# First key weights loaded in two halves over both queues, and the last store split over two queues

## The chip, the cores and the metric

The kernel runs on one core of one Trainium2 chip. The metric is the device time of one execution in microseconds (us); lower is better. Each kernel was run several times and the median is what counts. Besides, one execution was recorded by the hardware profiler, and every row shown below comes from that one.

## The reference

Three residual blocks are applied to x, 256 rows of 512 values. The first is a cross attention over 4096 context rows, and only its beginning matters here:

```python
x = x + xattn(layernorm(x), ctx_2048, mask, Wq, bq, Wk, bk, Wv, bv, Wo, bo, gamma, beta, residual_scale)
x = x + latent_attention(layernorm(x), ...)       # 16 heads, causal
x = x + mixture_of_experts(layernorm(x), ...)     # 48 kept experts, top 8 per row

# in xattn, hs = layernorm(x), at = ctx_2048:
q = proj(hs, Wq, bq, S)
k = proj(at, Wk, bk, T)      # at @ Wk.T + bk
v = proj(at, Wv, bv, T)
```

The last block's result, added to x, is the output: 256 x 512 float32, stored as two tiles of 128 rows.

## The kernel before

Every engine has its own hand-written program, and semaphores order the work between them: `sp` (SyncE) issues most transfers, `act` (ScalarE) and `dve` (VectorE) convert and combine, `pool` (GpSimd) makes constants and does the power for the layernorm, `pe` (TensorE) multiplies. Products of float32 quality are made of three float16 products: each operand is split into a high and a low part (`wk16[:, 0]` and `wk16[:, 1]` for the key weights, `chi` and `clo` for the context), and PE adds high x high (k = 0), low x high (k = 1) and high x low (k = 2).

The start of the program, which most of the change touches, computes the keys of the first 512 context rows. The contraction over 512 channels is cut into four chunks c = 0 to 3 of 128. For each chunk SP loads the key weights `wk32[:, c]` (256 KB, line 301) and ACT's own queue loads the context `cbuf[:, 0, c]` (256 KB, line 451); both count on one semaphore, `first_in[c]`. SP's queue also carries x (512 KB, line 300, ahead of the fourth key weights), and behind them the query weights, the value weights and the next context block, 1 MB each. When `first_in[c]` is full:

- ACT makes the high part of the key weights (line 471, `wk_hi`) and, from c = 1, that of the context (line 448, `ctx_hi`). For c = 0 DVE makes the latter (line 794).
- DVE makes the low parts, that of the weights (line 790, `wk_lo`) and that of the context (line 780, `ctx_lo`), chunk by chunk for c = 0, 1, 2. Behind these it computes the layernorm statistics of x (lines 800 to 802), POOL takes the power (line 416), DVE makes the low parts of chunk 3 and then the normalised x (`xn`, line 807).
- PE first runs ten products of zeros (`zero16`) that nothing reads. Then for each chunk and each of k = 0, 1, 2 it runs four matmuls of 512 columns, one for each group n of 128 key channels, into four PSUM banks (pP, pD and the two of pO): 48 in all. Ahead of the last four, those of c = 3, k = 2, it transposes `xn` (line 1280). Then come the query projection, the values of the first block, and the attention loop.

At the end of the program the experts' sum lies in two PSUM banks. DVE copies the first to `work[:, 0]` and ACT the second to `work[:, 1]` (line 766); SP stores each with one transfer of 256 KB (lines 378 and 380) and waits for both. Matmuls go through the helper of line 1268, so most of PE's rows carry that line.

Of the kernel before, what the change touches and what calls it, by code (L numbers as in the profile page):

```python
# [13 lines left out]
TT, HC = T // 128, HID // 128  # L14
# [18 lines left out]
SA, SW, SH = 64.0, 256.0, 16.0  # L33
# [14 lines left out]
def build(nc, a, out):  # L48
    f32, f16, i32 = mybir.dt.float32, mybir.dt.float16, mybir.dt.int32
    ALU, ACT, AX = mybir.AluOpType, mybir.ActivationFunctionType, mybir.AxisListType  # L50

    ctx = ExitStack()
    with ctx:
        def sb(name, shape, dt=f32):
            return ctx.enter_context(nc.sbuf_tensor(name, shape, dt))

        def sem(name):
            return ctx.enter_context(nc.semaphore(name))
# [7 lines left out]
        def unit_bank(b, n):  # L66

            if isinstance(b, int) and b == 0:
                return (pP[:, :], pD[:, :], pO[:, 0, :], pO[:, 1, :])[n % 4]
            return pP[:, :]  # L70
# [10 lines left out]
        work = sb("work", [128, 2, HID])  # L81
# [38 lines left out]
        def take(n, dt=f32):  # L120
            words = n if dt == f32 else n // 2
            v = arena[:, at[0]:at[0] + words]
            at[0] += words
            assert at[0] <= ARENA
            return v if dt == f32 else v.bitcast(dt)


        cbuf = take(2 * HC * CB).rearrange("p (b c t) -> p b c t", b=2, c=HC)
# [3 lines left out]
        wk16 = take(2 * HC * HID, f16).rearrange("p (s c n) -> p s c n", s=2, c=HC)  # L132
# [15 lines left out]
        wk32, wv32 = (take(HC * HID).rearrange("p (c n) -> p c n", c=HC) for _ in range(2))  # L148
# [96 lines left out]
        wdram = nc.dram_tensor("w_scratch", [KEPT, T], f32, kind="Internal").ap()  # L245


        names = """x_in small_in row_in wq_in wv_in wo_in gate_in lat_in rope_in
            aux_in var_ready rstd_ready xn_ready tr_done xT_ready
            zero_ready const_ready zc_ready prep_ready wk_hi wk_lo wq_hi wq_lo xq_hi xq_lo q_mm q_f q_hi q_lo  # L250
            ctx_hi ctx_lo proj_done proj_evac k_lo
# [9 lines left out]
        s = {n: sem(n) for n in names}  # L261
        first_in = [sem(f"first_in{i}") for i in range(HC)]
# [11 lines left out]
        def _(sp):  # L274
# [23 lines left out]
            for c in range(HC):  # L298
                if c == HC - 1:
                    sp.dma_start(x_sb[:, :, :], a["x"]).then_inc(s["x_in"], 16)  # L300
                sp.dma_start(wk32[:, c], a["wkT"][:, c]).then_inc(first_in[c], 16)
            sp.dma_start(wqT, a["wqT"]).then_inc(s["wq_in"], 16)
            sp.dma_start(wv32, a["wvT"]).then_inc(s["wv_in"], 16)
            load_ctx(1, 1)
# [72 lines left out]
            sp.wait_ge(s["out0_ready"], 1)  # L377
            sp.dma_start(out[:, 0, :], work[:, 0, :]).then_inc(s["out_stored"], 16)
            sp.wait_ge(s["out1_ready"], 1)
            sp.dma_start(out[:, 1, :], work[:, 1, :]).then_inc(s["out_stored"], 16)  # L380
            sp.wait_ge(s["out_stored"], 32)


        @block.gpsimd
# [61 lines left out]
        def _(act):  # L446
            def split_ctx(p, c):
                act.activation(chi[:, p, c], cbuf[:, p, c], ACT.Copy, scale=SA).then_inc(s["ctx_hi"], 1)

            for c in range(HC):  # L450
                act.dma_start(cbuf[:, 0, c], a["ctxT"][0][:, c]).then_inc(first_in[c], 16)

            def evac(b, p, n):

# [12 lines left out]
                                   scale=1.0 / (SA * SW)).then_inc(s["proj_evac"], 1)  # L467

            for c in range(HC):
                act.wait_ge(first_in[c], 32)  # L470
                act.activation(wk16[:, 0, c], wk32[:, c], ACT.Copy, scale=SW).then_inc(s["wk_hi"], 1)  # L471
                if c == 1:
                    act.wait_ge(s["ctx_hi"], 1)
                if c:
                    split_ctx(0, c)
# [6 lines left out]
            for i in range(2):  # L482
                act.activation(xqh[:, 2 * i:2 * i + 2, :], pS[:, i, :].rearrange("p (c t) -> p c t", c=2), ACT.Copy,
                               scale=SA).then_inc(s["xq_hi"], 1)
# [116 lines left out]
            for t in range(TT):  # L601
                act.wait_ge(s["tr_done"], t + 2)
                act.activation(xh[:, :, 128 * t:128 * t + 128], pS[:, t, :].rearrange("p (c q) -> p c q", c=HC), ACT.Copy,
                               scale=SX).then_inc(s["xT_ready"], 1)
# [126 lines left out]
            for t in range(TT):  # L731
                cols = slice(128 * t, 128 * t + 128)
                rows = pS[:, 2 + t, :].rearrange("p (c q) -> p c q", c=HC)
# [30 lines left out]
            moe_units(UNITS // UNROLL - 1, last_turn=True)  # L764
            act.wait_ge(s["moe_done"], 2)
            act.activation(work[:, 1, :], pP[:, :], ACT.Copy, scale=1.0 / (SH * SW)).then_inc(s["out1_ready"], 1)


        @block.vector
        def _(dve):  # L770
# [15 lines left out]
                dve.tensor_tensor(kl[:, p, n], kf[:, n % 2], kh[:, p, n], ALU.subtract).then_inc(s["k_lo"], 1)  # L786

            def split_wk(n):
                dve.wait_ge(s["wk_hi"], n + 1)
                dve.scalar_tensor_tensor(wk16[:, 1, n], wk32[:, n], SW, wk16[:, 0, n], ALU.mult, ALU.subtract)\  # L790
                   .then_inc(s["wk_lo"], 1)

            dve.wait_ge(first_in[0], 32)
            dve.tensor_scalar(chi[:, 0, 0], cbuf[:, 0, 0], SA, None, ALU.mult).then_inc(s["ctx_hi"], 1)
            for n in range(HC - 1):
                split_wk(n)
# [24 lines left out]
                dve.scalar_tensor_tensor(xql[:, 2 * i:2 * i + 2, :], pS[:, i, :].rearrange("p (c t) -> p c t", c=2), SA,  # L821
                                         xqh[:, 2 * i:2 * i + 2, :], ALU.mult, ALU.subtract).then_inc(s["xq_lo"], 1)
            for c in range(HC):
                dve.wait_ge(s["wk_hi"], HC + c + 1)
                dve.scalar_tensor_tensor(wv16[:, 1, c], wv32[:, c], SW, wv16[:, 0, c], ALU.mult, ALU.subtract)\
                   .then_inc(s["wk_lo"], 1)
            for n in range(HC):
# [438 lines left out]
        def _(pe):  # L1266
            def mm(o, lhsT, rhs, start, stop, **kw):
                return pe.matmul(o, lhsT, rhs, start=start, stop=stop, **kw)  # L1268
# [7 lines left out]
            def transpose_rows(k):  # L1276
                pe.wait_ge(s["xn_ready"], k)
                for t in range(TT):
                    for c in range(HC):
                        last = pe.transpose(pS[:, c // 2, 256 * (c % 2) + 128 * t:256 * (c % 2) + 128 * t + 128],  # L1280
                                            xn[:, t, 128 * c:128 * c + 128], ident[:, :])
                last.then_inc(s["tr_done"], 1)

            def unit_part(bank, p, n, c, products=(0, 1, 2)):

                for k, (wi, ci) in enumerate(((0, chi), (1, chi), (0, clo))):
                    if k not in products:
                        continue
                    start, stop = c == 0 and k == 0, c == HC - 1 and k == 2
                    if n < HC:  # L1290
                        last = mm(bank, wk16[:, wi, c, 128 * n:128 * n + 128], ci[:, p, c, :], start, stop)
                    else:
                        r = n - HC
                        last = mm(bank, ci[:, p, c, 128 * r:128 * r + 128], wv16[:, wi, c, :], start, stop)
                if c == HC - 1 and 2 in products:
                    last.then_inc(s["proj_done"], 1)
# [24 lines left out]
                    tiled_part(p, n, c)  # L1321

            pe.wait_ge(s["zero_ready"], 1)
            for _ in range(10):
                mm(pS[:, 0, :], zero16[:, 0:128], zero16[:, :], True, True)
            for c in range(HC):
                for k in range(3):
                    if k == 0:
                        pe.wait_ge(s["wk_hi"], c + 1)
                        pe.wait_ge(s["ctx_hi"], c + 1)  # L1330
                    elif k == 1:
                        pe.wait_ge(s["wk_lo"], c + 1)
                    else:
                        pe.wait_ge(s["ctx_lo"], c + 1)
                    if c == HC - 1 and k == 2:
                        pe.wait_ge(s["const_ready"], 1)
                        transpose_rows(1)
                    for n in range(HC):
                        unit_part(unit_bank(0, n), 0, n, c, (k,))
            for k, (w, x) in enumerate(((wqh, xqh), (wql, xqh), (wqh, xql))):  # L1340
                for g in range(HC):
# [531 lines left out]
```

## Time and profile before

| | us |
|---|---|
| median of 3 runs | 715.83 |
| lowest and highest of them | 715.80, 716.37 |
| the profiled execution, its own time | 716.18 |
| its span, from the first to the last instruction | 714.3 |
| what lies around its span | 1.88 |

The profile is read from the page's busy shares first, then by the chain of waits and by the instructions in order of time in the first 25 us and the last 5 us, where the change is. Times in those views are us from the start of the span.

### The profile page before, as it was taken

How to read it: one execution, taken by the hardware profiler on the slowest of the kernel's cores; microseconds unless marked ns; L12 is line 12 of the kernel's file. 1: busy time of each engine (PE TensorE's matmuls, PEld its weight loads, DVE VectorE, ACT ScalarE, POOL GpSimd, SP SyncE). 2: the span in 40 equal slices, each digit the busy share in tenths (PEclk: the TensorE clock that was granted, in tenths of full speed). 3: DMA queues.
4: the chain of work that ended last, by engine and by line, in shares of the span. 5: the costliest groups of instructions: out<-in, count | busy, mean ns of one | idle time of the engine just before them, and what ended most of it. 6: DMA issues, size and time to landing. Idle time of an engine off the chain costs nothing.

```text
span 714.3 us, 20505 instructions
## 1 busy us (share of the span) xinstructions
PE 700.1 (98%) x8725; PEld 455.7 (64%) x8725; DVE 610.9 (86%) x950; ACT 439.0 (61%) x610; POOL 11.6 (2%) x36
## 2 busy tenths in 40 slices
PE   8999999999999998998999999999999999999998
PEld 3555555555555554546777767777777777777775
DVE  5679999999999999877889977888888888888885
ACT  4778888787878887735677753444444344444442
POOL 3000000000000000010000000000000000000000
PEclk9999999999999999999999999999999999999999
DMA  8570101010110000032334403678777776777770
GB/s 322 175 276 3 62 3 62 3 61 10 54 25 39 3 3 3 3 128 98 112 121 155 161 1 105 224 215 250 220 246 222 242 239 227 245 225 243 230 238 32
DMA packets 29880, 94.44 MB, mean 132 GB/s; under 512 B 5824, under 2 KB 15088, under 8 KB 28400
## 3 DMA queue, kind: packets, MB, share of 16 engines
q1 hardware_dynamic: 28944, 92.31, 39.2%
q8 instruction: 57, 0.93, 0.6%
q10 hardware_dynamic: 864, 1.07, 0.4%
q14 instruction: 15, 0.12, 0.1%
HBM read 92.76 MB, written 0.57 MB: 131 GB/s over the span
## 4 chain that ended last, share of the span: by engine, by line
PE 91%; ACT 3%; DVE 3%; DMA 1%; issue 1%; POOL 0%; ACTq 0%; DVEq 0%
PE pS L1268 40%; PE pP L1268 30%; PE pO L1268 12%; PE pD L1268 8%; ACT arena L577 2%; DMA arena<-in_ctxT 1%; PE pO L1657 1%; ACT arena L618 0%; DVE xn L1183 0%; DVE xn L807 0%; POOL arena L439 0%; DVE bn L800 0%; DVE arena L1075 0%; DVE arena L790 0%; DVE arena L780 0%
## 5 line engine op out<-in xcount | busy, mean ns | idle before, releaser
L1268 PE MATMUL pS<-arena 128*128 128x256 f16 (+3 forms) x2185 | 253.5, 272 | 1.4 <-ACT arena L708 0.5
L1268 PEld LDWEIGHTS pS<-arena 128*128 128x128 f16 (+1 forms) x2185 | 213.4, 101 | 45.5 <-ACT arena L625 1.9
L1268 PE MATMUL pP<-arena 128*32 128x512 f16 (+1 forms) x2996 | 239.8, 380 | 0.2 <-ACT arena L471 0.2
L1268 PEld LDWEIGHTS pP<-arena 128*32 128x32 f16 (+1 forms) x2996 | 109.0, 97 | 102.0 <-issue 2.2
L531 ACT ACTIVATE arena<-pS,mblk 128x1024 f32<-128x1024 f32 x112 | 128.9, 1206 | 4.9 <-PE pS L1268 4.7
L1094 DVE SCALAR_TENSOR_TENSOR arena<-arena 128x1536 f16<-128x1536 f32 x72 | 126.1, 1752 | 0.8 <-ACT arena L687 0.8
L729 ACT ACTIVATE arena<-pS 128x256 f32<-128x256 f32 x72 | 27.6, 383 | 154.2 <-PE pS L1268 154.2
L1268 PE MATMUL pO<-arena 128*32 128x256 f32 (+6 forms) x1370 | 106.6, 357 | 1.7 <-DVE arena L1080 1.4
L687 ACT ACTIVATE arena<-arena 128x1536 f16<-128x1536 f32 x72 | 106.3, 1477 | 1.0 <-PE pP L1268 1.0
L936 DVE TENSOR_SCALAR arena<-arena 128x1024 f32<-128x1024 f32 x112 | 73.1, 689 | 7.0 <-ACT arena L531 7.0
L1268 PE MATMUL pD<-arena 128*128 128x512 f16 x288 | 77.8, 379 | 0.0
L1268 PEld LDWEIGHTS pO<-arena 128*32 128x32 f32 (+3 forms) x1370 | 47.4, 106 | 39.0 <-issue 15.5
L1229 DVE TENSOR_TENSOR arena<-pS,arena 128x256 f32<-128x256 f32 x72 | 30.6, 425 | 36.4 <-ACT arena L729 36.4
L1268 PE MATMUL pS<-work,arena 32*128 32x256 f16 x1536 | 53.4, 269 | 3.5 <-ACT arena L577 3.1
L1268 PEld LDWEIGHTS pS<-work,arena 32*128 32x128 f16 x1536 | 33.8, 93 | 32.8 <-issue 26.2
L1268 PEld LDWEIGHTS pD<-arena 128*128 128x128 f16 x288 | 28.2, 98 | 17.1 <-DVE arena L1242 0.2
L1238 DVE TENSOR_TENSOR arena<-arena 128x256 f32<-128x256 f32 x68 | 29.0, 426 | 7.1
L460 ACT ACTIVATE arena<-pP,xb 128x512 f16<-128x512 f32 x29 | 19.9, 687 | 24.3 <-PE pP L1268 24.3
L945 DVE TENSOR_TENSOR x_sb<-x_sb,arena 128x1024 f32<-128x1024 f32 x26 | 31.8, 1223 | 1.7 <-DVE x_sb L945 0.5
L945 DVE TENSOR_TENSOR arena<-arena 128x1024 f32<-128x1024 f32 x26 | 31.8, 1223 | 1.4
L945 DVE TENSOR_TENSOR xT<-xT,arena 128x1024 f32<-128x1024 f32 x26 | 31.8, 1222 | 1.4
L945 DVE TENSOR_TENSOR xn<-xn,arena 128x1024 f32<-128x1024 f32 x26 | 31.8, 1222 | 1.4
(260 smaller groups left out, 527.9 us busy)
## 6 DMA issues: line engine op xcount, KB each, us to landing
arena<-in_units SPq DMA_DIRECT2D x72, 768.0 KB, 5.0
arena<-w_scratch SPq DMA_DIRECT2D x136, 64.0 KB, 2.7
arena<-in_ctxT SPq DMA_DIRECT2D x7, 1024.0 KB, 5.3
mw_in<-in_mla_in SPq DMA_DIRECT2D x8, 832.0 KB, 6.8
mw_out<-in_mla_out SPq DMA_DIRECT2D x8, 512.0 KB, 3.8
wlatT<-in_wlatT SPq DMA_DIRECT2D x1, 1280.0 KB, 10.7
arena<-in_wkT SPq DMA_DIRECT2D x4, 256.0 KB, 5.4
arena<-in_ctxT ACTq DMA_DIRECT2D x4, 256.0 KB, 6.4
```

The lines of the kernel that those rows point to most:

```text
L460: act.activation(kh[:, p, n], bank, ACT.Identity, bias=xb[:, 1, n:n + 1], scale=1.0 / SW)
L531: act.activation(probs[:, tile], step_scores(st), ACT.Exp, bias=mblk[:, p, 1, tile:tile + 1], scale=mblk[:, p, 0, tile:tile + 1])\
L577: act.activation(probs[:, tile], step_scores(st), ACT.Exp, bias=mblk[:, p, 1, tile:tile + 1], scale=mblk[:, p, 0, tile:tile + 1])\
L687: act.activation(uwh[:, slot], uw32[:, slot], ACT.Copy, scale=SW).then_inc(s["unit_hi"], 1)
L729: act.activation(sg[:, buf], pS[:, bank, 0:T], ACT.Silu, scale=1.0 / (SA * SW)).then_inc(s["silu_ready"], 1)
L936: dve.tensor_scalar(probs[:, t], probs[:, t], LO, HI, ALU.max, ALU.min).then_inc(s["clip_done"], 1)
L945: dve.tensor_tensor(acc, acc, probs[:, t], ALU.add).then_inc(s["sum_done"], 1)
L1094: dve.scalar_tensor_tensor(uwl[:, slot], uw32[:, slot], SW, uwh[:, slot], ALU.mult, ALU.subtract).then_inc(s["unit_lo"], 1)
L1229: dve.tensor_tensor(m1[:, buf], pS[:, bank, T:2 * T], sg[:, slot], ALU.mult).then_inc(s["m1_ready"], 1)
L1238: dve.tensor_tensor(m2[:, buf], m1[:, buf], wb[:, slot], ALU.mult).then_inc(s["m2_ready"], 1)
L1268: return pe.matmul(o, lhsT, rhs, start=start, stop=stop, **kw)
L1657: last = pe.transpose(pO[:, j, 128 * i:128 * i + 128], pm[:, j, 128 * i:128 * i + 128], ident[:, :])
```

## The change

SP's loads of chunk 0 become three: the first 256 output channels of the key weights (128 KB, 1 KB of each partition), the partitions 96 to 127 of the first context chunk (64 KB), and the other 256 channels of the key weights (128 KB), the last on a semaphore of its own. ACT's queue loads only the partitions 0 to 95 of the first context chunk (192 KB). ACT converts the key weights of chunk 0 in two halves; PE begins the groups n = 0, 1 on the first half and waits for the second ahead of n = 2. Seven products of zeros stand where ten were. At the end, the second tile's store is cut by partitions into two of 128 KB: SP issues that of partitions 0 to 63, ACT that of 64 to 127.

```diff
             for c in range(HC):
                 if c == HC - 1:
                     sp.dma_start(x_sb[:, :, :], a["x"]).then_inc(s["x_in"], 16)
-                sp.dma_start(wk32[:, c], a["wkT"][:, c]).then_inc(first_in[c], 16)
+                if c:
+                    sp.dma_start(wk32[:, c], a["wkT"][:, c]).then_inc(first_in[c], 16)
+                    continue
+                sp.dma_start(wk32[:, 0, 0:256], a["wkT"][:, 0, 0:256]).then_inc(first_in[0], 16)
+                sp.dma_start(cbuf[96:128, 0, 0], a["ctxT"][0][96:128, 0]).then_inc(first_in[0], 16)
+                sp.dma_start(wk32[:, 0, 256:512], a["wkT"][:, 0, 256:512]).then_inc(s["wk_rest_in"], 16)
...
             sp.wait_ge(s["out1_ready"], 1)
-            sp.dma_start(out[:, 1, :], work[:, 1, :]).then_inc(s["out_stored"], 16)
-            sp.wait_ge(s["out_stored"], 32)
+            sp.dma_start(out[0:64, 1, :], work[0:64, 1, :]).then_inc(s["out_stored"], 16)
+            sp.wait_ge(s["out_stored"], 48)
...
             for c in range(HC):
-                act.dma_start(cbuf[:, 0, c], a["ctxT"][0][:, c]).then_inc(first_in[c], 16)
+                rows = slice(0, 96 if c == 0 else 128)
+                act.dma_start(cbuf[rows, 0, c], a["ctxT"][0][rows, c]).then_inc(first_in[c], 16)
...
             for c in range(HC):
-                act.wait_ge(first_in[c], 32)
-                act.activation(wk16[:, 0, c], wk32[:, c], ACT.Copy, scale=SW).then_inc(s["wk_hi"], 1)
+                act.wait_ge(first_in[c], 32 if c else 48)
+                if c == 0:
+                    act.activation(wk16[:, 0, 0, 0:256], wk32[:, 0, 0:256], ACT.Copy, scale=SW).then_inc(s["wk_hi"], 1)
+                    act.wait_ge(s["wk_rest_in"], 16)
+                    act.activation(wk16[:, 0, 0, 256:512], wk32[:, 0, 256:512], ACT.Copy, scale=SW).then_inc(s["wk_hi"], 1)
+                else:
+                    act.activation(wk16[:, 0, c], wk32[:, c], ACT.Copy, scale=SW).then_inc(s["wk_hi"], 1)
...
             act.activation(work[:, 1, :], pP[:, :], ACT.Copy, scale=1.0 / (SH * SW)).then_inc(s["out1_ready"], 1)
+            act.wait_ge(s["out1_ready"], 1)
+            act.dma_start(out[64:128, 1, :], work[64:128, 1, :]).then_inc(s["out_stored"], 16)
...
-            for _ in range(10):
+            for _ in range(7):
                 mm(pS[:, 0, :], zero16[:, 0:128], zero16[:, :], True, True)
             for c in range(HC):
                 for k in range(3):
                     if k == 0:
-                        pe.wait_ge(s["wk_hi"], c + 1)
+                        pe.wait_ge(s["wk_hi"], c + 2 if c else 1)
                         pe.wait_ge(s["ctx_hi"], c + 1)
...
                     for n in range(HC):
+                        if c == 0 and k == 0 and n == 2:
+                            pe.wait_ge(s["wk_hi"], 2)
                         unit_part(unit_bank(0, n), 0, n, c, (k,))
```

The other counts on `wk_hi` go up by one, since chunk 0 now adds two, and DVE's first wait on `first_in[0]` is for 48.

SP's program at its start, before the change; `arena` holds `wk32`, `cbuf` and the other weights, and the words in brackets are the semaphores waited for:

```order
L273 UNCONDITIONAL_BRANCH [waits barrier_Pool_Activation_PE_DVE_SP_release]
L301 DMA arena<-in_wkT 128x512 x3
L300 DMA x_sb<-in_x 128x1024
L301 DMA arena<-in_wkT 128x512
L302 DMA arena<-in_wqT 128x2048
```

And after it:

```order
L273 UNCONDITIONAL_BRANCH [waits barrier_Pool_Activation_PE_DVE_SP_release]
L304 DMA arena<-in_wkT 128x256
L305 DMA arena<-in_ctxT 32x512
L306 DMA arena<-in_wkT 128x256
L302 DMA arena<-in_wkT 128x512 x2
L300 DMA x_sb<-in_x 128x1024
L302 DMA arena<-in_wkT 128x512
L307 DMA arena<-in_wqT 128x2048
```

One transfer has become three, so two more stand ahead of the key weights of chunks 1 to 3 and of x.

PE's program at its start, before the change:

```order
L1268 MATMUL pS<-zero 128x512 [waits zero_ready]
L1268 MATMUL pS<-zero 128x512 x9
L1268 MATMUL pP<-arena 128x512 [waits ctx_hi,wk_hi]
L1268 MATMUL pD<-arena 128x512
L1268 MATMUL pO<-arena 128x512 x2
L1268 MATMUL pP<-arena 128x512 [waits wk_lo]
```

And after it:

```order
L1281 MATMUL pS<-zero 128x512 [waits zero_ready]
L1281 MATMUL pS<-zero 128x512 x6
L1281 MATMUL pP<-arena 128x512 [waits ctx_hi,wk_hi]
L1281 MATMUL pD<-arena 128x512
L1281 MATMUL pO<-arena 128x512 [waits wk_hi]
L1281 MATMUL pO<-arena 128x512
L1281 MATMUL pP<-arena 128x512 [waits wk_lo]
```

Three products of zeros are gone and the third real matmul has a wait of its own; the order of the real ones is the same.

## Rows read from the trace of the kernel before

**Rows 1.** The page's busy time of PE, and the shares of the chain that ended last.

```profile
span 714.3 us, 20505 instructions
PE 700.1 (98%) x8725; PEld 455.7 (64%) x8725; DVE 610.9 (86%) x950; ACT 439.0 (61%) x610; POOL 11.6 (2%) x36
PE 91%; ACT 3%; DVE 3%; DMA 1%; issue 1%; POOL 0%; ACTq 0%; DVEq 0%
```

**Rows 2.** Chain that ended last, first 30 us: start, duration, what.

```profile
1.73 7.74 DMA arena<-in_ctxT
...
9.49 0.64 ACT arena L471
...
10.15 0.69 DVE arena L790
10.85 0.60 DVE arena L780
11.45 0.62 DVE bn L800
...
14.62 1.40 DVE xn L807 x2
16.02 0.14 issue
16.15 1.07 PE pS L1280 x8
```

**Rows 3.** PE in order of time, its start: start, duration, instruction, idle before.

```profile
1.38 4.11 PE L1268 MATMUL pS<-zero 128*128 128x512 f16 x10 [1.38 <-POOL zero L393]
...
4.34 0.15 PEld L1268 LDWEIGHTS pS<-zero 128*128 128x128 f16 x1 [0.28 <-issue]
4.77 0.15 PEld L1268 LDWEIGHTS pS<-zero 128*128 128x128 f16 x1 [0.28 <-issue]
5.65 0.10 PEld L1268 LDWEIGHTS pP<-arena 128*128 128x128 f16 x1 [0.72 <-ACT arena L471]
5.65 0.39 PE L1268 MATMUL pP<-arena 128*128 128x512 f16 x1 [0.17 <-ACT arena L471]
...
14.51 0.38 PE L1268 MATMUL pD<-arena 128*128 128x512 f16 x1
14.73 0.59 PE L1268 MATMUL pO<-arena 128*128 128x512 f16 x2
```

**Rows 4.** ACT and DVE in order of time, chunk 0.

```profile
2.92 1.28 ACT L471 ACT_TABLE_LOAD   x1 [2.92 <-issue]
4.97 0.43 DVE L794 TENSOR_SCALAR arena<-arena 128x512 f16<-128x512 f32 x1 [4.97 <-DMA arena<-in_ctxT]
4.97 0.63 ACT L471 ACTIVATE arena<-arena 128x512 f16<-128x512 f32 x1 [0.76 <-DMA arena<-in_ctxT]
```

**Rows 5.** Issues of chunk 0, then of chunk 2, to landing.

```profile
arena<-in_wkT SPq DMA_DIRECT2D x1, 256.0 KB, 3.6
arena<-in_ctxT ACTq DMA_DIRECT2D x1, 256.0 KB, 4.1
...
1.25 0.90 SPq L301 DMA_DIRECT2D arena<-in_wkT  x2
arena<-in_wkT SPq DMA_DIRECT2D x1, 256.0 KB, 6.3
```

**Rows 6.** ACT's queue up to 7.5 and up to 8.0 us: packets, MB, share.

```profile
q10 hardware_dynamic: 391, 0.73, 28.2%
q10 hardware_dynamic: 432, 0.80, 29.1%
```

**Rows 7.** Issue and landing of x.

```profile
2.19 0.64 SPq L300 DMA_DIRECT2D x_sb<-in_x  x1
x_sb<-in_x SPq DMA_DIRECT2D x1, 512.0 KB, 8.2
```

**Rows 8.** The end of the program, 711.0 to 714.3 us: engines, transfers, GB/s in 40 slices.

```profile
711.15 0.60 ACT L766 ACTIVATE work<-pP 128x512 f32<-128x512 f32 x1 [3.50 <-PE pP L1268]
711.77 0.34 SPq L380 DMA_DIRECT2D out<-work  x1
GB/s 0 0 0 0 0 0 0 0 0 0 0 0 25 298 348 397 372 372 397 397 397 348 397 397 397 397 397 348 397 224 50 0 0 0 0 0 0 0 0 0
out<-work SPq DMA_DIRECT2D x1, 256.0 KB, 2.2
```

More of the change, by code:

```diff
@@ L245, in build @@
         wdram = nc.dram_tensor("w_scratch", [KEPT, T], f32, kind="Internal").ap()
-        names = """x_in small_in row_in wq_in wv_in wo_in gate_in lat_in rope_in
+        names = """x_in wk_rest_in small_in row_in wq_in wv_in wo_in gate_in lat_in rope_in
             aux_in var_ready rstd_ready xn_ready tr_done xT_ready
@@ L788, in split_wk @@
             def split_wk(n):
-                dve.wait_ge(s["wk_hi"], n + 1)
+                dve.wait_ge(s["wk_hi"], n + 2)
                 dve.scalar_tensor_tensor(wk16[:, 1, n], wk32[:, n], SW, wk16[:, 0, n], ALU.mult, ALU.subtract)\
                    .then_inc(s["wk_lo"], 1)
-            dve.wait_ge(first_in[0], 32)
+            dve.wait_ge(first_in[0], 48)
             dve.tensor_scalar(chi[:, 0, 0], cbuf[:, 0, 0], SA, None, ALU.mult).then_inc(s["ctx_hi"], 1)
@@ L823, in _ @@
             for c in range(HC):
-                dve.wait_ge(s["wk_hi"], HC + c + 1)
+                dve.wait_ge(s["wk_hi"], HC + c + 2)
                 dve.scalar_tensor_tensor(wv16[:, 1, c], wv32[:, c], SW, wv16[:, 0, c], ALU.mult, ALU.subtract)\
```

## The prediction

> **What bounds the kernel now.** The page comes first [rows 1]: PE is busy for 700.1 of 714.3 us, and 91% of the chain that ended last is PE. So nearly every microsecond by which PE's first real work moves is carried to the end, but only if PE is not held again behind it. The change touches nothing between the start and the last store, so the sum has two terms: how much sooner PE enters its steady work, and how much sooner the last store lands.
>
> At the start the tempting place is PE's first real matmul. PE runs zeros from 1.38 us and its first real matmul stands at 5.65, released by ACT's conversion [rows 3], which began at 4.97 when the first context chunk landed [rows 4]. But the chain of waits doesn't go through that matmul [rows 2]. It follows the transfer of the context chunk 2 from 1.73 to 9.47, ACT's conversion at 9.49, DVE's low parts at 10.15 and 10.85, the layernorm statistics from 11.45, the normalised x at 14.62, and PE's transposes at 16.15. Where does PE stand when the transposes become possible? Its last row ahead of them holds two matmuls from 14.73 [rows 3]. One of 512 columns takes 14.73 - 14.51 = 0.22 us, so PE would be free at 14.73 + 2 x 0.216 = 15.16. From 5.65 to 15.16 it has run 44 matmuls at 0.216 = 9.5 us: it hasn't waited at all. Then it waits for 16.15 - 15.16 = 0.99 us for the normalised x. That is the fact on which the forecast rests: **whatever PE gains at 5.65 only lengthens the wait ahead of 16.15. Time is gained only if chunk 2 lands sooner.**
>
> **The change, part by part.**
>
> *Chunk 0.* Before, its key weights land 3.6 us and its context 4.1 us after an issue at 0.8 [rows 5], the later at 4.91. What must land now is 128 + 64 KB on SP's queue and 192 KB on ACT's, where 256 and 256 were. The context's 4.1 us holds a part that doesn't shrink; the nearest row for it is the last store, 256 KB in 2.2 us with 1.4 us of data for both stores together, 0.7 for this one [rows 8], so about 1.5. The other 2.6 us shrink to three quarters, 1.95: the chunk would land at about 0.81 + 1.5 + 1.95 = 4.3. Bounds: ACT's table load ends at 4.20 [rows 4], and unchanged is 4.9. I take 4.4. ACT's half conversion lies between half of 0.63 and 0.63; I take 0.4, and PE starts at about 4.9 instead of 5.65. The second half lands behind 320 KB of SP's queue, at some 5.0, is converted by 5.4, and DVE's low part takes 0.7 more, to 6.1. PE's k = 1 then begins near 6.2, where 5.65 + 4 x 0.216 = 6.51 stood. PE's stream is 0.3 us ahead; if the second half is late by 0.3 it is level. **Worth on the path: 0**, since the wait at 16.15 covers it. With that cover gone it would be 0.3.
>
> *Chunk 2, the gate.* Its key weights land at 1.25 + 0.90 / 2 = 1.7, plus 6.3, that is 8.0 [rows 5]; its context at 9.47. ACT's queue is behind. The change takes 64 KB from ACT's queue and gives them to SP's. ACT's queue passes 0.80 - 0.73 = 0.07 MB in 0.5 us there [rows 6], so 64 KB (0.066 MB) are 0.47 us. The context of chunk 2 would land at 9.0. Its weights move the other way by as much, to 8.5 at most, and two more issues of 0.45 us each put them at 8.9 if issue were what holds them. Bounds: no move at all (the landing lags its data, which were through at about 7.9 [rows 6], by 1.5 us, and a lag needn't move), and 8.5, nearly 1.0 earlier, where the weights take over. I take 0.4, a little under the 0.47 of the row, because SP's queue now carries more and smaller packets beside it.
>
> *What follows.* ACT and DVE work on chunk 2 starts 0.4 earlier and so do the statistics, if x is there. x lands at 2.19 + 8.2 = 10.4 [rows 7], with 64 KB more ahead up to 10.9 at worst; the statistics would begin at 11.45 - 0.4 = 11.05. That cap is at 10.9, a gain of 0.55. The transposes move to 15.75, and PE, free at about 14.9, still waits for them. **Worth: 0.4 us, between 0 and 0.55.**
>
> *Seven products of zeros.* Seven at 4.77 - 4.34 = 0.43 us end at 1.38 + 3.0 = 4.4, ten at about 5.6, so with ten the real matmul at 4.9 would queue behind them. The page grants full clock throughout, yet zeros stand 0.43 apart and real matmuls 0.22: 512 columns are at 1.2 GHz in the first and 2.4 in the second. The rise falls between the load of 0.15 us at 4.77 and that of 0.10 us at 5.65 [rows 3], with PE busy before it. Now PE pauses from 4.4 to 4.9. If the rise stays put, at most two or three real matmuls take 0.43 instead of 0.22, 0.4 us, inside the slack. **Worth: 0.** The Trainium skill (TensorE: Matmul & The Clock Gate, "What's actually happening") says that the low clock is the default and activity lifts it, which speaks against taking activity away; that is the slower rival below.
>
> *The last store.* ACT writes the tile until 711.75, SP issues at 711.77, and it lands 2.2 later. Data flows without a gap from slice 13 to slice 30 of the 40 (0.0825 us each), near 397 GB/s, as the two stores follow one another [rows 8]. A second queue shortens only the issue of 0.34 us, by at most 0.17, and that issue lies beside data of the first store. ACT's issue could be slower: at the start its transfer landed 0.5 after SP's of the same size [rows 5]. Bounds +0.17 gained, 0.5 lost. **I take 0**, as engines that are full are the nearest row. The Trainium skill (DMA: Bandwidth & Descriptors, "Rules for kernel authors") says of transfers to disjoint partition halves not to bother, for both halves use the same engines. It speaks against both splits; applied to the loads it would make the gain 0, and the continuous rate at the end agrees with it for the store.
>
> Sum against the profiled execution: 716.18 - 0.4 = 715.8. That execution is 0.35 above the median of the runs, so for a median: 715.83 - 0.4 = **715.4**.
>
> **The rivals.**
>
> 1. *Gain that doesn't arrive.* The landing of chunk 2 keeps its place, since the 1.5 us between data and landing may come from one late engine, or because the engines share the same bytes between the queues in another order. Then the transposes stand at 16.15 and the time is 715.8. For it: the same 2.5 MB must pass by then. Against it: ACT's queue does have 64 KB less ahead. 0.27. (The skill's rule on halves is this rival.)
> 2. *More than forecast.* Chunk 2 at 8.5, capped by x, 0.55 to 0.7, and 0.17 of the issue at the end: 715.83 - 0.8 = 715.0. 0.13.
> 3. *The clock stays low.* The pause at 4.4 delays the rise. Each us at 1.2 GHz costs PE 0.5 us of its stream. PE has 0.99 of slack and 0.3 of earlier start; a rise 2.6 us late, at about 8, is free, and from there it costs. [...] To be slower by over 0.2% it must rise later than 2 x (1.43 + 1.3) = 5.5 us after its old place, at about 11 us. For it: the zeros are the only activity ahead. Against it: seven of ten remain and real work follows within 0.5 us. 0.06 for up to 716.3, 0.02 beyond 717.3.
> 4. *SP's queue becomes the gate.* Key weights of chunk 2 or 3, or x, land 1 us later: x from 10.4 to 11.9 would cost 0.45, and ACT's issue 0.2 at the end: 716.2. Against it: 64 KB are worth under 0.5. 0.06.
>
> **How the numbers follow.** The forecast has 0.46. A measurement of this kernel can tell 0.2% from no change, 1.43 us. No case but the far end of rival 3 reaches that on the slow side; on the fast side all terms at their best give under 1. I leave 0.05 for a faster and 0.04 for a slower result by something not in these rows (loops that settle otherwise), and 0.91 for the same. The range 714.9 to 716.2 reaches from the sum of the best terms to the first cost of rivals 3 and 4.
>
> **What would show it.** In the changed profile: ACT's first conversion near 4.4 and PE's first real matmul near 4.9, with real matmuls 0.22 apart from about 5.5 (else rival 3); ACT's conversion of chunk 2 at 9.1 (9.5 is rival 1, 8.6 rival 2); the statistics at once behind DVE's low parts and not behind x (else rival 4); a wait of about 1 us ahead of the transposes, now at 15.75; the query products 0.4 earlier and that lead kept to the end; the last landing still 2.2 us after ACT's last copy. I am wrong if PE has no wait ahead of the transposes, or if the end moves by more than the transposes do.

## The result

The changed kernel is slower: a median of 718.96 us over 6 runs (718.62 to 720.1) against 715.82 us for the kernel before, measured beside it (715.69 to 716.37). The ratio is 1.0045, with a 95% interval of 1.0032 to 1.0058. The forecast was 715.4, in a range of 714.9 to 716.2. (To be exact about the title: both halves of the key weights stand in SP's queue; what is spread over both queues is the first context chunk.)

The profiled execution took 718.62 us, and its span grew from 714.3 to 716.7. The page of the changed kernel has PE busy for 701.1 us where 700.1 stood, so of the 2.4 us 1.0 is longer work and 1.4 is waiting. The longer work is in the first real matmuls, which take 0.43 us each instead of 0.22, less three zeros that are gone. The page's busy times:

```profile
span 716.7 us, 20503 instructions
PE 701.1 (98%) x8722; PEld 455.4 (64%) x8722; DVE 610.8 (85%) x950; ACT 439.5 (61%) x611; POOL 11.6 (2%) x36
```

The chain of waits over the first 40 us of the changed kernel (start, duration, what) answers to [rows 2]:

```profile
1.71 0.43 SPq L306
2.14 0.04 issue
2.18 7.59 DMA arena<-in_wkT
9.80 0.63 ACT arena L482
10.43 0.53 ACT arena L453
10.95 0.14 issue
11.09 0.38 PE pP L1281
...
17.72 0.43 PE pO L1281 x2
18.16 0.87 PE pS L1293 x8
```

The chain has changed its road. It no longer goes through chunk 2's context and the layernorm; it goes through the **key weights of chunk 1**, which SP issues at 2.18 and which are there at 2.18 + 7.59 = 9.77. ACT then converts the weights and the context, and PE starts chunk 1 at 11.09. From there to the transposes it runs 32 matmuls of 0.216 us, 6.9 us, without a wait: 11.09 + 6.9 = 18.0. The transposes stood at 16.15 before, and the wait of 0.99 us ahead of them is used up. Before, PE went on to chunk 1 at 5.65 + 12 x 0.216 = 8.24; now it does so 2.85 us later, which is the slack of 0.99 and 1.86 more. What SP and ACT issued, by size and time to landing, one row for each of SP's first four transfers in order:

```profile
arena<-in_wkT SPq DMA_DIRECT2D x1, 128.0 KB, 2.9
arena<-in_ctxT SPq DMA_DIRECT2D x1, 64.0 KB, 3.5
arena<-in_wkT SPq DMA_DIRECT2D x1, 128.0 KB, 4.5
arena<-in_wkT SPq DMA_DIRECT2D x1, 256.0 KB, 7.6
```

The first three, issued at 0.80, 1.25 and 1.71, land at 3.7, 4.7 and 6.2. PE and ACT in order of time show what chunk 0 got from it:

```profile
4.77 0.42 ACT L478 ACTIVATE arena<-arena 128x256 f16<-128x256 f32 x1 [0.79 <-DMA arena<-in_ctxT]
5.37 0.59 PE L1281 MATMUL pP<-arena 128*128 128x512 f16 x1 [0.83 <-DVE arena L807]
6.27 0.42 ACT L480 ACTIVATE arena<-arena 128x256 f16<-128x256 f32 x1 [1.08 <-DMA arena<-in_wkT]
8.00 0.15 PEld L1281 LDWEIGHTS pO<-arena 128*128 128x128 f16 x1 [0.28 <-issue]
8.43 0.15 PEld L1281 LDWEIGHTS pO<-arena 128*128 128x128 f16 x1 [0.28 <-issue]
9.68 0.10 PEld L1281 LDWEIGHTS pO<-arena 128*128 128x128 f16 x1 [0.25 <-issue]
```

PE's first real matmul comes at 5.37 instead of 5.65 [rows 3], and ACT's second half can't begin before 6.27. The loads of 0.15 us, 0.43 apart, until past 9.28 are TensorE at 1.2 GHz, after a pause; before, the loads were 0.10 us long from 5.65 on. (The page's row of the granted clock shows full clock there in both kernels, so the level is read from the spacing.)

At the end, the last store is issued by both engines at 713.57. Its issues last longer than the 0.34 us of [rows 8], and the landings come 2.4 and 2.7 us after them instead of 2.2:

```profile
713.57 0.53 SPq L385 DMA_DIRECT2D out<-work  x1
713.57 0.56 ACTq L779 DMA_DIRECT2D out<-work  x1
...
out<-work SPq DMA_DIRECT2D x1, 128.0 KB, 2.4
out<-work ACTq DMA_DIRECT2D x1, 128.0 KB, 2.7
```

From ACT's last copy to the end of the span it is 716.7 - 712.94 = 3.8 us, before 714.3 - 711.15 = 3.15. So of the 2.4 us about 1.8 come from the start (the copy began at 712.94 instead of 711.15) and 0.6 from the store.

### The profile page after: what moved, and what is told of

It reads as the page before. It is cut to its first block, busy times and chain, and to the rows that moved or that the text cites. A ratio compares the mean times of both kernels' runs of the same rounds, so it can differ in the third digit from the quotient of the medians.

```text
span 716.7 us, 20503 instructions
## 1 busy us (share of the span) xinstructions
PE 701.1 (98%) x8722; PEld 455.4 (64%) x8722; DVE 610.8 (85%) x950; ACT 439.5 (61%) x611; POOL 11.6 (2%) x36
## 4 chain that ended last, share of the span: by engine, by line
PE 92%; ACT 3%; DVE 2%; DMA 1%; issue 1%; POOL 0%; SPq 0%; DVEq 0%
PE pS L1281 40%; PE pP L1281 30%; PE pO L1281 13%; PE pD L1281 8%; ACT arena L588 2%; DMA arena<-in_wkT 1%; PE pO L1672 1%; ACT arena L629 0%; DVE xn L1196 0%; POOL arena L444 0%; DVE arena L1088 0%; DVE arena L1046 0%; ACT arena L614 0%; DVE arena L1050 0%; DVE arena L1013 0%
## 6 DMA issues: line engine op xcount, KB each, us to landing
wlatT<-in_wlatT SPq DMA_DIRECT2D x1, 1280.0 KB, 10.7
```

## The experiments

Every kernel below was timed beside the kernel before on the same chip, whose medians lay between 716.02 and 716.09; beside the changed kernel it was 715.82. All compute the whole result.

**The parts of the change.** The last store alone:

```diff
-            sp.dma_start(out[:, 1, :], work[:, 1, :]).then_inc(s["out_stored"], 16)
-            sp.wait_ge(s["out_stored"], 32)
+            sp.dma_start(out[0:64, 1, :], work[0:64, 1, :]).then_inc(s["out_stored"], 16)
+            sp.wait_ge(s["out_stored"], 48)
...
+            act.wait_ge(s["out1_ready"], 1)
+            act.dma_start(out[64:128, 1, :], work[64:128, 1, :]).then_inc(s["out_stored"], 16)
```

> The kernel before with only the last store split over the two queues. Theory: the two issues at the same moment get in each other's way, and the last landing comes 2.7 us after ACT's last copy instead of 2.2; the end moves by +0.5 to +0.6 us, a time of about 716.4. Rival: the longer end of the changed kernel was one execution's scatter, or came from the late start; then the end is 2.2 us after the copy and the time 715.8.

Measured 716.67, ratio 1.0009 (1.0000 to 1.0018), landings at 2.4 and 2.7 us. (Ten executions lay between 716.45 and 717.04, one took 906.28.) The store costs 0.65 in the median, an interval that touches zero. Its profiled execution says the same: from ACT's last copy to the end it is 714.5 - 710.76 = 3.7 us, where 3.15 stood.

The changed kernel with the store put back:

> The changed kernel with the last store as it was before: one transfer on SP's queue. Theory: the start costs 1.8 us of the span by itself, with the key weights of chunk 1 landing near 9.8 us, and the time is about 718.3 (the change's median less 0.6). Rival: if the start is only a part and the split store costs more than 0.6 in the median run, the time is 717.5 or less.

Measured 718.77, ratio 1.0046 (1.0032 to 1.0059), from 718.62 to 720.07. The start alone costs 2.75, more than the 1.8 in the changed kernel's profiled execution. Here the profiled execution lost 2.5 us (a span of 716.8 against 714.3): chunk 1's key weights landed at 10.3 instead of 9.8, the second half of chunk 0's at 7.1 instead of 6.2, and PE, at 1.2 GHz from 8.5 on, reached chunk 1 at 11.64, just as its conversions ended. So the late second half and the clock are a limit as close as chunk 1.

The same with ten products of zeros (`range(7)` back to `range(10)`):

> As head_only, but with ten products of zeros again. Theory that the late key weights of chunk 1 are the gate: PE has to wait for them near 11 us whatever its clock, so this is equal to head_only within 0.3 us. Rival, the clock: PE's rate rises near 5.5 us again and not near 9.5 us, and the time is 1 us or more lower than that of head_only.

Measured 718.51, 0.26 under head_only. TensorE is at 2.4 GHz from 7.6 us on, finishes chunk 0 and waits for chunk 1, whose key weights land at 10.2; PE starts on it at 11.54, 0.1 earlier than in head_only. The clock isn't what makes the changed start slow. What it is worth there, 5 and 6 executions that scatter by 1.5 and 1.7 us can't tell.

Only the zeros changed, in the kernel before:

> The kernel before with seven products of zeros instead of ten and nothing else. If the pause ahead of the first real matmul keeps TensorE at its lower clock until about 9.5 us, PE's first twelve real matmuls take 0.43 us each: up to 12 x 0.21 = 2.6 us of its stream lost, 0.99 of it covered by the wait for the transposes, so up to +1.6 us and a time of 716.5 to 717.4. If the clock rises where it did, the time is 715.8.

Measured 717.01, ratio 1.0014 (1.0005 to 1.0023), from 715.73 to 717.89. The profiled execution was the one of 715.73: weight loads of 0.10 us from the first real one. So it was run once more:

> seven_zeros once more, for a profile of a slower execution: its times scattered from 715.7 to 717.9 and the profiled one was the fastest. If the scatter is the clock, an execution above 717 shows weight loads of 0.15 us, 0.43 apart, past 6 us; if it is the loads, they are 0.10 us from the first real one and the chunks land later.

Measured 716.79, ratio 1.0010 (1.0000 to 1.0020), from 716.03 to 717.68. Now the profiled execution took 717.68, and the later transfer of each chunk landed within 0.25 us of where it lands before. Weight loads in order of time:

```profile
9.45 0.15 PEld L1268 LDWEIGHTS pO<-arena 128*128 128x128 f16 x1 [0.28 <-issue]
9.88 0.15 PEld L1268 LDWEIGHTS pO<-arena 128*128 128x128 f16 x1 [0.28 <-issue]
10.30 0.15 PEld L1268 LDWEIGHTS pP<-arena 128*128 128x128 f16 x1 [0.28 <-ACT arena L471]
10.63 0.10 PEld L1268 LDWEIGHTS pD<-arena 128*128 128x128 f16 x1 [0.18 <-issue]
```

The rise stands near 10.5 us instead of ahead of 5.67. Three zeros fewer leave PE idle from 4.4 to 5.6 in this kernel, and some executions pay up to 1.9 us for it, others nothing. The clock is a real cost of its own, 0.7 to 1.0 in the median. The 1.95 us between the two profiled executions aren't all clock, though: in the fast one chunk 2's context came at 8.98 and the transposes at 15.66, where the kernel before had 9.47 and 16.15. With the same loads, landings scatter by 0.5 us and more.

**What makes chunk 1 late.** I held it to be the packets of 1 KB, with the number of transfers as the rival. Chunk 0's key weights by two transfers, converted together, cut by columns and then by rows:

```diff
+                if c == 0:
+                    sp.dma_start(wk32[:, 0, 0:256], a["wkT"][:, 0, 0:256]).then_inc(first_in[0], 16)
+                    sp.dma_start(wk32[:, 0, 256:512], a["wkT"][:, 0, 256:512]).then_inc(first_in[0], 16)
+                    continue
                 sp.dma_start(wk32[:, c], a["wkT"][:, c]).then_inc(first_in[c], 16)
```

```diff
+                if c == 0:
+                    sp.dma_start(wk32[0:64, 0], a["wkT"][0:64, 0]).then_inc(first_in[0], 16)
+                    sp.dma_start(wk32[64:128, 0], a["wkT"][64:128, 0]).then_inc(first_in[0], 16)
+                    continue
                 sp.dma_start(wk32[:, c], a["wkT"][:, c]).then_inc(first_in[c], 16)
```

> The kernel before with the key weights of chunk 0 loaded by two transfers on SP's queue, each half of the columns of every partition (packets of 1 KB), converted together as before. Theory 'packets': SP's queue falls behind ACT's while it passes packets of half the size, the key weights of chunk 1 land after 7.5 us instead of 5.75, and the time is 0.5 to 2 us above the kernel before (716.5 to 718). Rival 'issues': only the number of transfers counts; then this and weights_by_rows cost the same, 0.5 us at most each.

> The same number of transfers as weights_by_columns, but cut by partitions 0 to 63 and 64 to 127, so that packets keep their 2 KB. Theory 'packets': equal to the kernel before, 716.0, within 0.4 us, with the key weights of chunk 1 at about 5.8 us. Rival 'issues': as late as weights_by_columns.

Measured 717.76 and 717.28, ratios 1.0024 (1.0014 to 1.0033) and 1.0031 (1.0021 to 1.0041). (The second ratio is above that of the medians, 1.0017, since its executions reach from 716.90 to 720.28.) Chunk 1's key weights land at 9.3 and 8.9. Packets of 2 KB didn't save it: my theory fell, and so did the size that I gave its rival, at most 0.5 us.

Only the first context chunk over both queues:

```diff
+                if c == 0:
+                    sp.dma_start(cbuf[96:128, 0, 0], a["ctxT"][0][96:128, 0]).then_inc(first_in[0], 16)
...
-                act.dma_start(cbuf[:, 0, c], a["ctxT"][0][:, c]).then_inc(first_in[c], 16)
+                rows = slice(0, 96 if c == 0 else 128)
+                act.dma_start(cbuf[rows, 0, c], a["ctxT"][0][rows, c]).then_inc(first_in[c], 16)
```

> The kernel before with only the first context chunk cut: 96 partitions on ACT's queue, 32 on SP's behind the whole key weights. Packets stay at 2 KB, 64 KB move from one queue to the other. Theory 'packets': no harm, chunk 2's context 0 to 0.5 us sooner, a time of 715.5 to 716.0. Rival, that the 64 KB and the one more issue on SP's queue are what makes the later weights late: 716.5 or more.

Measured 717.62, ratio 1.0025 (1.0015 to 1.0034): as costly again. The same cut at chunk 2 (`c == 2` in both places), where the added transfer stands behind chunk 1's and chunk 2's weights:

> A candidate for a better version: the kernel before, with chunk 2's context cut 96 to 32 partitions over the two queues, behind SP's key weights of chunk 2, since there ACT's queue lands last (9.47 us against 8.0). If that context is the gate of the start, it lands near 9.0 and the time is 0.3 to 0.5 us lower than before, 715.6. Rival: SP's queue is as late as ACT's once it carries more, and the time is 716.0 or above.

Measured 715.88, ratio 0.9998 (0.9989 to 1.0007): not to be told from before. Its profiled execution has chunk 2's context at 8.8 instead of 9.47 and the transposes at 15.50 instead of 16.15, as I had forecast for the change. But seven_zeros had 8.98 and 15.66 with its loads untouched, so a gain isn't shown. Nor does this added transfer, fourth in SP's queue, do harm: chunk 3's key weights land at 11.1 (11.3 before) and x at 10.5 (10.4).

A transfer with hardly any bytes, 0.5 KB, behind chunk 0's key weights:

```diff
                 sp.dma_start(wk32[:, c], a["wkT"][:, c]).then_inc(first_in[c], 16)
+                if c == 0:
+                    sp.dma_start(rs[:, :], a["rs"].broadcast_to([128, 1])).then_inc(s["aux_in"], 16)
```

> The kernel before with one transfer of 0.5 KB (the residual scale, which is loaded later anyway) issued on SP's queue between the key weights of chunks 0 and 1. It adds an issue and next to no bytes. If a further transfer ahead is what makes chunk 1 late, whatever it carries, the key weights of chunk 1 land after 8 us and the time is 717 or more. If the bytes or the split of one chunk over two transfers does it, they land at about 6.0 and the time is 716.1, within 0.4.

Measured 718.53, ratio 1.0036 (1.0022 to 1.0050), chunk 1's key weights at 10.2. Neither bytes nor the split of a chunk are needed. (SP's issue of chunk 3's key weights takes 2.53 us here and 1.78 in the changed kernel, 0.46 before. It comes behind that of chunk 1, so it isn't the cause.)

Is it what SP issues behind chunk 1? Two kernels hold that back. The changed start with the large transfers waiting for chunk 1 (`sp.wait_ge(first_in[1], 32)` ahead of the query weights), and tiny_ahead with everything from chunk 2 on waiting for chunk 0 (`sp.wait_ge(first_in[0], 32)` at c == 2):

> The changed start (head_only) with SP waiting for the whole of chunk 1 before it issues the query weights and what is behind them, 3 MB in all. If these large transfers, issued while chunk 1 is under way, are what slows it, its key weights land below 7.5 us (10.4 in head_only), even if the query weights then come late themselves. If not, they land at about 10 us and the time is that of head_only, 718.8, or more.

> tiny_ahead with SP waiting for chunk 0 to land (near 5 us) before it issues the key weights of chunk 2 and all behind them. If what SP issues behind chunk 1 is what keeps it late, its key weights land below 7.5 us (10.1 in tiny_ahead) and the time is at least 1 us under tiny_ahead's 718.5. If the small transfer ahead does it by itself, they land near 10 us still.

Measured 718.73 and 717.46. Chunk 1's key weights land at 9.9 and 9.6. So neither the three large transfers nor anything issued behind chunk 1 before 4.78 us is the cause; chunk 2, chunk 3 and x are still issued before it lands. In head_big_later's profiled execution, the slowest of five, PE doesn't even wait for chunk 1: the second half of chunk 0 lands at 7.5 and TensorE is at 1.2 GHz until 13.5. (tiny_hold is 1.1 below tiny_ahead all the same; their profiled executions were both among the slowest of their kernels, with the clock falling to 1.2 GHz after a wait of 3 us, and don't tell why.)

Is it SP's queue, or the place? The small transfer on ACT's queue behind its chunk 0, and on SP's one place later (`c == 1`):

> The small transfer on ACT's queue, between the context of chunks 0 and 1. If a queue's third transfer is the late one whichever queue it is, chunk 1's context lands after 8 us and the time is 717 or more. If only SP's queue behaves so, chunk 1 lands near 6.5 and the time is 716.1, within 0.4.

> The small transfer on SP's queue one place later, behind the key weights of chunk 1. Place in the queue: chunk 1 lands at 5.7 as before, chunk 2's key weights near 10 instead of 8.0, and as its context lands at 9.4 anyway the time is 0.2 to 1 us above the kernel before. If the small transfer does harm wherever it stands (128 packets of 4 bytes), chunk 1 is late here too and the time is 718 or more.

Measured 718.49 and 717.17, ratios 1.0033 (1.0022 to 1.0043) and 1.0015 (1.0006 to 1.0024). On ACT's queue it makes chunk 1's context late (10.1), and SP's chunk 1 too (7.1). One place later it leaves chunk 1 alone (6.5; 5.7 to 6.4 with the loads untouched) and delays chunk 2's key weights to 10.7, from where the chain goes through the layernorm again.

Two kernels without an added transfer. Chunks 1 and 2 merged into one transfer on each queue (`wk32[:, 1:3]`, `cbuf[:, 0, 1:3]`), and the halves of the change with the second half in one transfer with chunk 1:

```diff
-                sp.dma_start(wk32[:, 0, 0:256], a["wkT"][:, 0, 0:256]).then_inc(first_in[0], 16)
-                sp.dma_start(cbuf[96:128, 0, 0], a["ctxT"][0][96:128, 0]).then_inc(first_in[0], 16)
-                sp.dma_start(wk32[:, 0, 256:512], a["wkT"][:, 0, 256:512]).then_inc(s["wk_rest_in"], 16)
+                elif c == 0:
+                    sp.dma_start(wk32[:, 0, 0:256], a["wkT"][:, 0, 0:256]).then_inc(first_in[0], 16)
+                else:
+                    flat, flat_in = (v.rearrange("p c n -> p (c n)") for v in (wk32, a["wkT"]))
+                    sp.dma_start(flat[:, 256:1024], flat_in[:, 256:1024]).then_inc(s["wk_rest_in"], 16)
```

> The kernel before with the key weights of chunks 1 and 2 as one transfer of 512 KB, second on SP's queue, and their context likewise on ACT's. If the place in the queue decides, both land near 6.5 to 7.5 us and the time is at or below that of the kernel before. If the bytes and the slow stretch decide, they land where chunk 2 landed, 8.0 and 9.4, chunk 1 with them; PE then waits for chunk 1 near 9.4 + 1.3 = 10.7, and the time is 1 to 1.5 us above before: 717.3.

> The halves of the change without a further transfer: SP loads the first 256 columns of chunk 0's key weights, then the rest of them together with chunk 1's as one transfer of 384 KB; the context stays on ACT's queue, ten products of zeros. If only the added transfers do the harm, chunk 1 lands below 7 us and the time is 716.1, within 0.4: no gain either, as chunk 2 is the gate. If packets of 1 KB or the second conversion do it, the time is 717 or more.

Measured 717.04 and 716.25, ratios 1.0013 (1.0004 to 1.0022) and 1.0003 (0.9994 to 1.0012). With the chunks merged the landings are at 8.7 and 7.6, neither of the two places that I gave; the time is near the second forecast. The other kernel shows what does no harm: halves, the second conversion, PE's wait in the middle of chunk 0 and packets of 1 KB are all in it, and it can't be told from the kernel before. What it lacks against head_ten_zeros, 2.3 us slower, is the two added transfers and the 64 KB moved with one of them; by tiny_ahead the bytes aren't needed. Its transfer of 384 KB, second in the queue, is there sooner than the 256 KB in the changed kernel:

```profile
arena<-in_wkT SPq DMA_DIRECT2D x1, 384.0 KB, 4.9
```

All of them in one table; landings are those of the profiled execution, rounded to 0.1 us:

| kernel | place of chunk 1 (SP, ACT) | chunk 1: weights, context | chunk 2: weights, context | median |
|---|---|---|---|---|
| before | 2, 2 | 5.7, 6.3 | 8.0, 9.5 | 715.82 |
| seven_zeros | 2, 2 | 6.4, 5.7 | 7.8, 9.0 | 717.01 |
| seven_zeros_again | 2, 2 | 6.4, 5.8 | 8.1, 9.5 | 716.79 |
| the change | 4, 2 | 9.8, 5.4 | 10.9, 8.0 | 718.96 |
| head_only | 4, 2 | 10.3, 5.2 | 11.5, 8.4 | 718.77 |
| head_ten_zeros | 4, 2 | 10.2, 5.2 | 11.3, 8.7 | 718.51 |
| head_big_later | 4, 2 | 9.9, 5.2 | 10.8, 8.2 | 718.73 |
| weights_by_columns | 3, 2 | 9.3, 5.6 | 10.6, 8.1 | 717.76 |
| weights_by_rows | 3, 2 | 8.9, 6.1 | 10.1, 7.2 | 717.28 |
| context0_both | 3, 2 | 9.4, 5.8 | 10.8, 8.5 | 717.62 |
| tiny_ahead | 3, 2 | 10.2, 5.9 | 11.5, 9.4 | 718.53 |
| tiny_hold | 3, 2 | 9.6, 5.6 | 11.0, 9.0 | 717.46 |
| tiny_act | 2, 3 | 7.1, 10.1 | 9.5, 12.0 | 718.49 |
| tiny_behind_chunk1 | 2, 2 | 6.5, 5.7 | 10.7, 8.8 | 717.17 |
| context2_both | 2, 2 | 6.3, 5.8 | 7.6, 8.8 | 715.88 |
| halves_no_more_transfers | 2, 2 | 6.2, 6.3 | 7.6, 9.1 | 716.25 |
| chunks_merged | 2, 2 | 8.7, 7.6 | with chunk 1 | 717.04 |

Every kernel whose chunk 1 was pushed to the third place of a queue or beyond has it at 8.9 us or later there, whatever the added transfer carried. Where it kept the second place in both queues and its size, it landed between 5.7 and 6.5. That an added transfer ahead makes it late is shown. The number of its place is not the whole rule: chunk 2's key weights, third behind 512 KB, land at 8.0 before the change, chunk 1's, third behind 256.5 KB, at 10.2 in tiny_ahead, and the changed kernel's own third transfer is there at 6.2. A full transfer of 256 KB as the one added was not tried, so it is open whether any transfer does it or only a short or narrow one.

**The stretch behind it.** Do the rates show where the time goes? The half microseconds from 6.0, first of the kernel before, then of tiny_behind_chunk1; the last two columns are the share of time in which the 16 DMA engines were busy, and GB/s:

```profile
6.00:6.50 0.50, 0.50 (x4) 0.19 (x2) 0.50 (x2) 0.19 (x1) 0.00 (x0) 1.00 0.98 238
6.50:7.00 0.50, 0.50 (x4) 0.24 (x3) 0.45 (x2) 0.50 (x2) 0.00 (x0) 1.00 0.91 225
```

```profile
6.00:6.50 0.50, 0.50 (x3) 0.26 (x4) 0.50 (x1) 0.00 (x1) 0.00 (x0) 1.00 0.28 49
6.50:7.00 0.50, 0.50 (x4) 0.20 (x3) 0.50 (x2) 0.50 (x1) 0.00 (x0) 1.00 0.48 78
```

Already before the change the engines were busy and yet moved only 217 to 238 GB/s from 6.0 to 7.5, where 381 to 467 went through from 8.0 on. With the small transfer the engines mostly stand idle from 6.0 to 7.0, while work waits in both queues. But this isn't what slows the changed kernel. Packets, MB and share of each queue in the first 8.0 us (q1 is SP's, q10 ACT's), before, in the changed kernel and in tiny_ahead:

```profile
q1 hardware_dynamic: 461, 0.91, 41.3%
q10 hardware_dynamic: 432, 0.80, 29.1%
```

```profile
q1 hardware_dynamic: 535, 0.71, 36.4%
q10 hardware_dynamic: 527, 0.96, 35.7%
```

```profile
q10 hardware_dynamic: 396, 0.74, 35.0%
q1 hardware_dynamic: 432, 0.54, 32.5%
```

Together the queues of the changed kernel moved 1.67 MB where 1.71 stood; SP's got less of it and ACT's more. In tiny_ahead the sum itself fell, to 1.27. Nor are the bytes the last word: up to the end of chunk 1 SP's queue of the changed kernel has 576 KB (0.59 MB) to pass, and it had passed 0.60 MB by 7.5, and yet chunk 1 wasn't complete until 9.77. Packets of 4 KB, which only x has, behind chunks 1 and 2, were under way from 7.54. So some of the queue's work ran ahead while some of chunk 1 was still missing. Before the change SP's queue had 512 KB (0.52 MB) up to there, had passed 0.51 MB by 5.25, and chunk 1's weights were complete at 5.72. Why the work of one queue drifts apart so, why the stretch is slow, and what an added transfer does to either, no run settles.

**The store.** Whole from ACT's queue, and cut by columns over both:

```diff
-            sp.dma_start(out[:, 1, :], work[:, 1, :]).then_inc(s["out_stored"], 16)
+            sp.dma_start(out[:, 1, 0:256], work[:, 1, 0:256]).then_inc(s["out_stored"], 16)
...
+            act.dma_start(out[:, 1, 256:512], work[:, 1, 256:512]).then_inc(s["out_stored"], 16)
```

> The kernel before with the last store issued whole by ACT, nothing by SP. If ACT's queue is slower by itself the landing is 2.6 us or more after the copy and the time 716.5; if only two issues at the same moment hinder each other, it is 2.2 us as SP's and the time 716.0.

> The last store cut by columns: 128 partitions of 1 KB on each queue, issued at the same moment. In the split by partitions the issues took 0.53 and 0.57 us, where a transfer of 128 partitions takes 0.35. If the form with 64 partitions is the cause, the issues take 0.35 here and the time is 716.1; if two queues at the same moment hinder each other, it is 716.6 as in tail_only.

Measured 716.18 and 716.23, ratios 1.0001 (0.9992 to 1.0010) and 1.0003 (0.9994 to 1.0012). From ACT's last copy to the end it is 714.1 - 710.88 = 3.2 us in the first and 714.4 - 710.99 = 3.4 in the second, against 3.15 before and 3.7 in tail_only. ACT's queue is hardly slower than SP's, and two issues at the same moment are not what costs 0.6. The issues of the kernel cut by columns:

```profile
711.62 0.34 SPq L380 DMA_DIRECT2D out<-work  x1
711.62 0.38 ACTq L768 DMA_DIRECT2D out<-work  x1
```

0.34 and 0.38 us for 128 partitions, where the cut by 64 partitions took 0.53 and 0.56. In weights_by_rows each issue of 64 partitions took 0.58 as well, while the 0.39 and 0.42 of the transfers of 128 and 32 partitions in the changed kernel are ordinary. At the store, the form with 64 partitions is what goes with the slow issue. (It is no measure for every issue: in weights_by_rows the next one, of 128 partitions, took 0.58 too.) The transfer rates over the end of the store by partitions, 40 slices of 0.1 us, also have a gap that the other stores lack, between the first tile's data and the second's. What makes the gap wasn't tested:

```profile
GB/s 0 0 0 0 0 0 0 0 0 0 0 102 328 369 348 389 451 389 226 21 102 184 266 184 164 225 143 287 348 471 205 41 0 0 0 0 0 0 0 0
```

## Why the prediction was wrong

Right was the frame: PE had no wait from 5.65 to 15.16 and 0.99 us of slack ahead of the transposes, an earlier first matmul gains nothing by itself, and what moves the transposes moves the end. In the changed kernel they moved by 1.8 to 2.0 us and ACT's last copy by 1.79. Both signs that I had named for being wrong came: no wait ahead of the transposes, and an end that moved by more than they did (2.4).

- **Chunk 0.** Forecast: landing at 4.4, PE at 4.9, second half converted by 5.4, worth 0. Measured: 4.77, 5.37 and 6.69. The sizes were off by 0.4 to 1.3 us, and with ten zeros that alone would still have cost nothing: halves_no_more_transfers has its second half hardly earlier (its conversion begins at 6.18 against 6.27) and equals the kernel before.
- **Chunk 2, the gate: the step that failed.** I priced two more transfers on SP's queue as two issues of 0.45 us and 64 KB, and applied that to chunk 2 and to x only. Chunk 1 stands in no term. Its key weights moved by 4.05 us, from 5.72 to 9.77, which took all slack and 1.8 us more. What an added transfer costs is not its issue and its bytes: tiny_ahead's 0.5 KB moved chunk 1 by 4.4 us. Why it costs so much stays open. Rival 4 had the right queue but a delay of 1 us (1.5 in its sum for x), for chunks 2 and 3 and x; x in fact went from 10.4 to 12.1.
- What I did forecast for chunk 2's context happened: it came from 9.47 to 7.95, earlier than the 9.0 that I took, but its weights came to 10.9, past the bound of 8.9 that I gave.
- **The zeros.** Forecast 0, with rival 3 at 0.08. By themselves they cost 0.7 to 1.0 in the median. In the changed start the late second half and chunk 1 hide most of that; head_ten_zeros is 0.26 lower, less than the scatter.
- **The store.** Forecast 0, bound 0.5 lost; measured 0.65 in the median and 0.6 in both profiled executions. I took full engines as the nearest row, and the profile has a gap in their work. The Trainium skill's advice to use one transfer of 128 partitions (DMA: Bandwidth & Descriptors, "Rules for kernel authors") gives the right sign here. In tail_columns_both two queues were no gain either. That halves by partitions are dearer than halves by columns is from the runs.

In sum the start's 2.75 and the store's 0.65 make 3.4, measured are 3.14; the difference is within the scatter of head_only's and the changed kernel's runs, 1.5 us each.

## What to carry to other kernels

At the start of a program, where everything is loaded at once, count transfers and not only bytes: here one more of them, of 0.5 KB, ahead of the second chunk cost 2.4 us in the median, while one of 64 KB in the fourth place cost nothing that could be measured. When a transfer is added, list everything behind it in its queue with the slack of its user, beginning with the next one, not with the one that bounds the kernel now. If halves are wanted, the second half can be joined with the transfer behind it, which cost nothing here (and gained nothing). A last store, if it must be cut, was cheaper by columns than into 64 partitions; at the start the cut by columns was no better than that by rows (717.76 and 717.28).

## What had not been expected of the hardware

- The DMA engines moved 217 to 238 GB/s from 6.0 to 7.5 us in the kernel before, at a busy share of 0.85 to 0.98, and 381 to 467 from 8.0 to 10.5; with a small transfer ahead of chunk 2 they fell to 49 at a share of 0.28 from 6.0 to 6.5.
- A transfer of 0.5 KB took 4.1 us from its issue to its landing behind chunk 0's key weights and 6.9 behind chunk 1's.
- In the changed kernel SP's queue had passed more bytes than chunk 1 needs 2.3 us before chunk 1 was complete.
- Issues of 64 partitions took 0.53 to 0.58 us, of 128 partitions 0.34 to 0.43 as a queue's first and at the store; with transfers queued ahead single issues of 128 partitions took up to 2.53.
- After a pause of 1.2 us behind seven zeros TensorE ran at 2.4 GHz at once in one profiled execution and at 1.2 until near 10.5 us in another, of the same kernel, with its chunks 0 and 1 landing within 0.1 us of each other.
